# Self entries of a graph aggregation: 63 products on TensorE replaced by ten adds on GpSimd

## The reference, cut to what matters

```python
x, src, dst = ...                     # x [1250, 512]; 40000 edges, ids below 1250
def gnn(x, edge_index, W1, b1, W2, b2):
    h = relu(x @ W1 + b1) @ W2 + b2   # W1 [512, 256], W2 [256, 512]
    row, col = edge_index             # (src, dst)
    agg = segment_sum(h[col], row, num_segments=1250)
    return h + agg                    # h itself: the self entry of each node
def ffn(x, W_gate, b_gate, W_thr, b_thr, W_exp, b_exp):   # 8 experts of 512 x 512
    g = softmax(x @ W_gate + b_gate)
    w = g - 0.25 * sigmoid(x @ W_thr + b_thr)
    w = where(w >= 0, w, 0); w = w / sum(w)               # 1 where the sum is 0
    return sum_e w[:, e] * (x @ W_exp[e] + b_exp[e])
x = x + gnn(layernorm(x), (src, dst), ...)
x = x + ffn(layernorm(x), ...)
```

## Time and profile before

| | before |
|---|---|
| median of 3 runs | 352.44 us (351.34 to 352.58) |
| profiled execution | 352.29 us |
| its span, first to last instruction | 350.4 us |
| PE busy | 338.0 us, 96% |
| DVE busy | 296.0 us, 84% |
| ACT busy | 119.7 us, 34% |
| POOL busy | 83.6 us, 24% |
| mean granted TensorE clock | 0.995 of full |

### The profile page before, as it was taken

How to read it: one execution, slowest core, us unless ns; L and a number is a source line. 1 busy time by engine, 2 the same in 40 slices (tenths; PEclk the granted TensorE clock), 3 DMA queues, 4 the chain that set the end, 5 groups by cost and what they waited for, 6 DMA issues and landing times.

```text
span 350.4 us, 7647 instructions
## 1 busy us (share of the span) xinstructions
PE 338.0 (96%) x2637; PEld 263.4 (75%) x2637; DVE 296.0 (84%) x571; ACT 119.7 (34%) x233; POOL 83.6 (24%) x151
## 2 busy tenths in 40 slices
PE   8699999999999999899999999999999999999995
PEld 8599885655555545567668888888888888888884
DVE  7799999997896869977878888888889888898764
ACT  6898753454542026577313121030030210300000
POOL 5000032434343003437324060320500502200000
PEclk9989999999999999999999999999999999999999
DMA  8965132334433400040000030210300300000133
GB/s 179 254 162 173 43 83 59 74 80 93 89 86 85 135 0 0 0 127 3 0 0 2 2 120 3 59 64 2 120 3 2 120 2 2 1 2 0 60 116 121
DMA packets 20226, 22.09 MB, mean 63 GB/s; under 512 B 11850, under 2 KB 12647, under 8 KB 20188
## 3 DMA queue, kind: packets, MB, share of 16 engines
q1 hardware_dynamic: 17420, 18.36, 18.8%
q0 software_dynamic: 2352, 2.71, 3.4%
q10 hardware_dynamic: 416, 0.53, 0.7%
HBM read 12.77 MB, written 2.56 MB: 44 GB/s over the span
## 4 chain that ended last, share of the span: by engine, by line
PE 86%; DVE 7%; issue 2%; DMA 2%; ACT 1%; DVEq 0%; SPq 0%; ACTq 0%
PE ps_g L1195 12%; PE ps_g L1394 11%; PE ps_g L1395 11%; PE ps_g L1396 11%; PE ps_w L1255 8%; PE ps_g L1183 5%; PE ps_a L1394 2%; PE ps_a L1396 2%; PE ps_a L1395 2%; PE ps_g L1318 2%; PE ps_w L1394 2%; PE ps_w L1395 2%; PE ps_w L1396 2%; PE ps_w L1234 2%; PE ps_g L1360 2%
## 5 line engine op out<-in xcount | busy, mean ns | idle before, releaser
L1067 DVE SCALAR_TENSOR_TENSOR x_sb<-ps_g,weight_s,x_sb 125x256 f32<-125x256 f32 (+1 forms) x142 | 75.2, 547 | 19.5 <-PE ps_g L1396 18.4
L865 DVE TENSOR_TENSOR split<-places,keys 125x756 f16<-125x756 int16 (+4 forms) x119 | 73.2, 675 | 4.8 <-PE ps_w L1255 2.5
L1394 PE MATMUL ps_g<-wb_hi,places 128*128 128x256 f16 x212 | 57.8, 273 | 0.1
L1395 PE MATMUL ps_g<-wb_lo,places 128*128 128x256 f16 x212 | 57.8, 273 | 0.0
L1396 PE MATMUL ps_g<-wb_hi,r_sb 128*128 128x256 f16 x212 | 57.8, 273 | 0.0
L1195 PE MATMUL ps_g<-late,r_sb 125*128 125x512 f32 (+3 forms) x120 | 51.7, 534 | 0.9 <-DMA late<-counts 0.9
L401 POOL DMA_DIRECT2D late<-counts x49 | 28.3, 577 | 80.5 <-ACT counts L599 80.0
L1255 PEld LDWEIGHTS ps_w<-split 125*128 125x128 f16 x476 | 29.9, 98 | 13.8 <-issue 6.4
L1394 PE MATMUL ps_g<-wb_hi,split 128*128 128x256 f16 x142 | 38.7, 273 | 0.0
L1396 PE MATMUL ps_g<-wb_hi,split 128*128 128x256 f16 x142 | 38.7, 273 | 0.0
L1395 PE MATMUL ps_g<-wb_lo,split 128*128 128x256 f16 x142 | 38.7, 273 | 0.0
(11 more groups left out here) (232 smaller groups left out, 679.5 us busy)
## 6 DMA issues: line engine op xcount, KB each, us to landing
stage<-in_L_ffn_W_exp_dram SPq DMA_DIRECT2D x8, 1024.0 KB, 5.2
late<-counts SPq DMA_DIRECT2D x54, 58.6 KB
late<-counts POOLq DMA_DIRECT2D x41, 58.6 KB, 2.8
x_sb<-in_x_dram SPq DMA_DIRECT2D x5, 448.0 KB, 11.2
out_dram<-x_sb SPq DMA_DIRECT2D x10, 224.0 KB
w_sb<-in_L_gnn_W_dram SPq DMA_DIRECT2D x2, 512.0 KB, 10.9
out_dram<-x_sb ACTq DMA_DIRECT2D x10, 26.0 KB
b_sb<-in_L_gnn_b_dram SPq DMA_DIRECT2D x1, 250.0 KB
```

The costliest lines, as they stand in the source:

```text
L865: nc.vector.tensor_tensor(hot[hot_at(stage, p)][:, 0:n, :].rearrange("p c (k x j) -> p c k x j", k=SEGS, j=2), places_of(windows[s], n), k ...
L1067: nc.vector.scalar_tensor_tensor(out=x_sb[:, i, a:z], in0=bank[0:R, at:at + z - a], scalar=weight_s[:, expert_of(u), i:i + 1], in1=x_sb[:, ...
L1394: nc.tensor.matmul(out_cols, hi_x, wb_hi[par][:, q, k, :], start=(opens and k == 0), stop=False, skip_group_check=True)
L1395: nc.tensor.matmul(out_cols, hi_x, wb_lo[par][:, q, k, :], start=False, stop=False, skip_group_check=True)
```

## The change

The bank of a group is opened by a product of zeros with one column, which only marks it as fresh (`clear`), and no self entries are counted. When a tile's rows have landed, GpSimd adds the identity to the 125 x 125 block of the tile that lies on the diagonal (`add_self`), for tiles 0 to 8 behind its own moves of group LAST[i] + 2 (tile 0: group 8), for tile 9 behind all moves. Cut 0 and `column_sum` wait for this add (`self_added`) in place of the landings; for tile 9 only cut 2, which holds the diagonal block, waits for it, and comes after cut 3. The constants `self_pos` and `self_lo` go.

```diff
-        self_pos = sb("self_pos", [128, 128 + HI - 1], F16)
-        self_lo = sb("self_lo", [128, 3 * LO + 2 * WIN], F16)
-        zeros = sb("zeros", [1, BANK], F16)
+        zeros = sb("zeros", [128, 128], F16)
+        SELF_LAG = 2
@@ GpSimd
-            nc.gpsimd.memset(zeros[:, :], 0.0).then_inc(self_ready, 1)
-            nc.gpsimd.memset(self_pos[:, :], 0.0).then_inc(self_base, 1)
-            nc.gpsimd.memset(self_lo[:, :], 0.0).then_inc(self_base, 1)
-            pool.wait_ge(self_base, 2)
-            pool.wait_ge(const_ready, CONSTS)
-            nc.gpsimd.tensor_tensor(self_pos[...], ident[...], ident[...], ALU.add).then_inc(self_ready, 1)
+            nc.gpsimd.memset(zeros[:, :], 0.0).then_inc(zeros_ready, 1)
+
+            def add_self(i):
+                moved(pool, i)
+                own = a_t[i % 3][:, i * R:(i + 1) * R]
+                nc.gpsimd.tensor_tensor(own, own, ident[0:R, 0:R], ALU.add).then_inc(self_added, 1)
...
+            SELF_AT = {max(LAST[i] + SELF_LAG, POOL_MOVES): i for i in range(TILES - 1)}
+            pool.wait_ge(const_ready, CONSTS)
             begun = [2]
             for g in range(POOL_MOVES, NG):
                 pool.wait_ge(win_out, g + 1)
                 move(pool, g, 1, begun)
+                if g in SELF_AT:
+                    add_self(SELF_AT[g])
+            add_self(TILES - 1)
@@ ScalarE
-            act.wait_ge(self_base, 2)
             act.wait_ge(const_ready, CONSTS)
-            for a in (0, WIN):
-                at = LO if a == 0 else 2 * LO + WIN
-                nc.scalar.activation(self_lo[...], ident[...], ACT.Copy).then_inc(self_ready, 1)
@@ VectorE
             def column_sum(i):
-                moved(dve, i)
+                dve.wait_ge(self_added, i + 1)
@@ TensorE
             def aggregate(i, first, last, closes=None):
                 if first == 0:
-                    moved(pe, i)
+                    pe.wait_ge(self_added, i + 1)
...
-            def self_entries(g, pieces):
...
+            def clear(g, pieces):
+                empty = nc.tensor.matmul(ps_w[g % 2][:, 0:1], zeros[:, :], zeros[:, 0:1], start=True, stop=False, skip_group_check=True)
                 if g > 0 and g - 1 not in pieces and (g > SLOTTED or last_step_of(g - 1) % SLOT_STEPS > 0):
-                    own.then_inc(win_done, 1)
-                if not whole:
-                    ...
+                    empty.then_inc(win_done, 1)
...
-                self_entries(g, pieces)
+                clear(g, pieces)
...
-            pe.wait_ge(self_ready, 4)
+            pe.wait_ge(zeros_ready, 1)
...
             moved(pe, TILES - 1)
-            begin = (0, 2, 3)
+            begin = (0, 3, 2)
             for n in begin:
+                if n == 2:
+                    pe.wait_ge(self_added, TILES)
                 g = cut(TILES - 1, n)
```

More of the change, by code:

```diff
@@ L252, in gnn_moe @@
         places_ready, pads_ready = sem("places_ready"), sem("pads_ready")
-        self_base, self_ready = sem("self_base"), sem("self_ready")
+        zeros_ready, self_added = sem("zeros_ready"), sem("self_added")
         keys_placed = sem("keys_placed")
@@ L504, in _ @@
             group_rows(fill, (row_inv, "inv"), (row_size, "size"), (row_base, "base"))
-            nc.gpsimd.memset(zeros[:, :], 0.0).then_inc(self_ready, 1)
-            nc.gpsimd.memset(self_pos[:, :], 0.0).then_inc(self_base, 1)
-            nc.gpsimd.memset(self_lo[:, :], 0.0).then_inc(self_base, 1)
-            pool.wait_ge(self_base, 2)
-            pool.wait_ge(const_ready, CONSTS)
-            nc.gpsimd.tensor_tensor(self_pos[0:2 * WIN, HI - 1 + SHIFT:HI - 1 + SHIFT + POS].rearrange("p (r h) -> p r h", h=HI)[:, :, 0],
-                                    ident[0:2 * WIN, 0:WIN], ident[0:2 * WIN, WIN:2 * WIN], ALU.add).then_inc(self_ready, 1)
+            nc.gpsimd.memset(zeros[:, :], 0.0).then_inc(zeros_ready, 1)
[3 more added lines that the diff above has]
+                nc.gpsimd.tensor_tensor(own, own, ident[0:R, 0:R], ALU.add).then_inc(self_added, 1)
             def block_sums(e):
@@ L524, in block_sums @@
                 nc.gpsimd.tensor_tensor(t_sum[:, T4 - T1, :, :], b21, t_sum[:, T2 - T1, :, :], ALU.subtract).then_inc(t_added, 1)
+            SELF_AT = {max(LAST[i] + SELF_LAG, POOL_MOVES): i for i in range(TILES - 1)}
+            assert len(SELF_AT) == TILES - 1 and max(SELF_AT) < NG
+            pool.wait_ge(const_ready, CONSTS)
             begun = [2]
@@ L616, in _ @@
                 table(k)
-            act.wait_ge(self_base, 2)
             act.wait_ge(const_ready, CONSTS)
-            for a in (0, WIN):
-                at = LO if a == 0 else 2 * LO + WIN
-                nc.scalar.activation(self_lo[0:2 * WIN, at:at + WIN], ident[0:2 * WIN, a:a + WIN], ACT.Copy).then_inc(self_ready, 1)
             key_view = keys[:, FRONT * REC:(FRONT + CH) * REC].rearrange("p (c t) -> p c t", t=REC)
@@ L1223, in slot_behind @@
                         turn_x(k + XTS)
-            def self_entries(g, pieces):
[L1227 to L1235, removed]
-                if g > 0 and g - 1 not in pieces and (g > SLOTTED or last_step_of(g - 1) % SLOT_STEPS > 0):
-                    own.then_inc(win_done, 1)
-                if not whole:
-                    a = 0 if rows <= WIN else LO
-                    nc.tensor.matmul(bank[:, a:cols], self_pos[:, HI - 2 - tile:HI - 2 - tile + 128],
-                                     self_lo[:, 2 * LO - at + a:2 * LO - at + cols], start=False, stop=False, skip_group_check=True)
+            def clear(g, pieces):
+                empty = nc.tensor.matmul(ps_w[g % 2][:, 0:1], zeros[:, :], zeros[:, 0:1], start=True, stop=False, skip_group_check=True)
+                if g > 0 and g - 1 not in pieces and (g > SLOTTED or last_step_of(g - 1) % SLOT_STEPS > 0):
+                    empty.then_inc(win_done, 1)
             def count(g, pieces):
```

## The result

The changed kernel is slower: median 356.06 us (355.9 to 356.33, 5 runs) against 352.44 us, ratio 1.0114 with a 95% interval of 1.01 to 1.0128. That is outside the range, and on the other side than forecast. Its profiled execution has a span of 354.3 us where before had 350.4.

What follows compares the result with a forecast made beforehand. TensorE was taken as the bound, with VectorE close behind. Removing products gives 3.15 us, less 0.95 and 0.2 for waits at tiles 4 and 5: 2.0 us, so 350.4 us against 352.44; range 349.2 to 353.0.

Steps and rivals of the forecast that it cites:

- tile 0's add: GpSimd in group 12: issued at about 46.9, waits out L922's 1.48 us, delays VectorE's next step 0.35 us; net gain 0.
- the rule that an add costs: GpSimd's adds: each costs VectorE up to 0.35 us and itself up to one step more, 0.66 us at group 12.
- Rival (c): Adds of tiles 4 to 8 starve behind VectorE's back-to-back steps, 5.5 us on TensorE's path: 355.9 us; chance 0.09.
- The removal of the products: TensorE from 52.8 us on: dropping the self-entry products saves 3.15 us, before the waits for adds are taken off.
- The 0.25 us taken off behind cuts of 512 columns: TensorE: work beside the fixed path falls from 1.47 to 1.36 us, just under it, so 0.25 us less gain over all.
- the one-column product: TensorE, opening each group's bank: taken at 0.057 us from L1342's rows, against 0.11 for L1234 in an ordinary group.
- Rival (b): The one-column product costs a full 0.11 us in ordinary groups, so 1.35 us saved: 351.1 us; chance 0.13.
- the removal gives nothing before 52.8 us: Groups 0 to 12: TensorE would save 1.2 us but VectorE never rests, so 0, between -0.3 and +0.3.
- The wait at tile 4: TensorE's first cut of tile 4 waits 1.1 us for landing plus add, 0.15 of it waited already: costs 0.95.
- Tile 5: TensorE's first cut of tile 5 waits for the add, ready at 90.0: costs 0.2 us.
- tile 9's add: In the tail: ready at about 117.8, hidden by a microsecond behind cuts 0 and 3, so it costs nothing.
- Rival (d): VectorE bounds groups 24 to 31 and 12, as adds cost it extra: 1 to 2 us back, 351.4 to 352.4; chance 0.17.

Runs made afterwards that it cites:

- e8: The kernel before with one GpSimd add of 125 x 125 on scratch behind GpSimd's move of group 8, nobody waiting for it: 351.83 us, ratio 1.0014.
- e2: The changed kernel with a VectorE memset of 512 columns of scratch behind each of the two L923 passes: 350.84 us, ratio 0.9971.
- e5: The changed kernel with a VectorE add of two SBUF inputs, 512 columns on scratch, behind each of the two L923 passes: 357.08 us, ratio 1.0137.
- e10: The changed kernel with each of the ten adds replaced by a GpSimd memset on scratch, same waits, self entries left out: 348.88 us, ratio 0.9906.
- e9: The kernel before with one GpSimd add on scratch behind the move of group 8, first waiting until tile 0 has landed: 357.2 us, ratio 1.0139.
- e7: The changed kernel with 18 products of ones on TensorE just ahead of its first wait for an add: 353.53 us, ratio 1.0037.
- e3: The changed kernel without the ten adds, waiting for landings as before the change, self entries left out: 348.72 us, ratio 0.9914.
- e6: The changed kernel with a one-column VectorE memset behind the one-hot steps of each group from 8 on: 349.68 us, ratio 0.9938.
- e11: The changed kernel with a one-column VectorE memset behind the one-hot steps of groups 8 to 29 only: 349.54 us, ratio 0.9924.

## Why the prediction was wrong

**The step that failed** is the one on tile 0's add: "it is issued at about 46.9, sits out the 1.48 us of L922 and then holds up the next step by its own length, 0.35 us", and with it the rule that an add costs "itself up to one step (0.66 us at group 12) more". I took it that the two engines take turns, from two pairs of instructions; there they did, and so did e8's add. Tile 0's was issued at 46.24 and sat out L923 and the 12 steps and the other L923 behind it, 10.93 us in place of under 2. VectorE's row was in the earlier trace rows, 12.80 busy of 12.80 us; I used it only for what the add would cost VectorE, not for when GpSimd would get in. e2 and e5 show that it waits for VectorE's two-input row, e10 that an instruction without reads doesn't, and e9 that neither the landed rows nor TensorE's wait is needed for it.

**Rival (c)** named the mechanism, an add that starves behind VectorE's back-to-back steps, and its 355.9 us lie beside the measured 356.06. That is luck in the number: it put the starving at tiles 4 to 8, where the adds took 0.40 to 0.74 us, and didn't price tile 0, nor the clock. It had a chance of 0.09. The reason against it, that VectorE is idle while it waits for the same add, did hold for tile 4; at tile 5 VectorE was in its last step and waited 0.34 us behind it. It is also a reason why one starved add was all: the adds of tiles 2 and 3 (70.60 and 78.07 us) came less than 0.6 us before VectorE stopped for a column sum that waits for them.

**The lowered clock** was in no part of the prediction: 2.25 us, shown by e7. The wait of 4.88 us on TensorE was dearer by this than its length.

**The removal of the products** came out right in sum: 3.15 us forecast, 3.1 measured (e3). Part of that is luck, since terms in it were off. The 0.25 us taken off behind cuts of 512 columns have no ground in the earlier trace rows: the work there, 1.36 us, is longer than the path from 92.64 to 93.88, which is 1.24. At tile 4 e3 waits 0.38 us for the bare landing, which the 3.15 don't hold. And the one-column product was too dear: it starts 0.03 us ahead of the first one-hot product, not 0.057, as the timeline of the changed kernel shows:

```profile
72.00 0.17 PE L1228 MATMUL ps_w<-zeros 128*128 128x1 f16 x1
72.03 0.60 PE L1244 MATMUL ps_w<-split 125*128 125x125 f16 x8
```

Rival (b), a one-column product at the full 0.11 us, is out. The weight load's length, which spoke for it, doesn't set the spacing: L1342's loads are longer (0.14 us) than L1234's (0.10), and still four of its products take 0.23 us. What took back what the cheaper product gave isn't shown; the waits behind the short cuts, which from 84.79 us on end with VectorE in e3, are the likely place.

**That the removal gives nothing before 52.8 us** was right: TensorE waited for VectorE in group 12, and the first cut of e3 came 0.09 us earlier.

**The wait at tile 4** was right in place and nearly in size: forecast 1.1 us, measured 0.81 in the changed kernel and in e2, and 0.89 in e6. With 0.38 of it in e3 too, the add itself accounts for about 0.4. The chain of the changed kernel has landing, add and cut in a row:

```profile
84.43 3.34 DMA late<-counts
87.77 0.41 POOL late L510
88.22 1.13 PE ps_g L1196 x2
```

The add is 0.41 us where 0.35 was taken. Tile 5 didn't wait (0.2 forecast); tile 9's add hid, as forecast, though it took 1.38 us.

**Rival (d)**, VectorE as the bound, showed late in the stage (waits of 0.48, 0.48 and 0.53 us for one-hots at 98.79, 105.69 and 112.64), but e3 has waits of the same size without any add, so it isn't the adds that cost them.

The forecast of 350.4 us is near what the change brings where no add starves: e11 has 349.54.

## What to carry to other kernels

Before work is put on GpSimd, look at what VectorE does at the moment when it arrives, not at what both do on the average: a GpSimd instruction that reads SBUF can be held off for as long as VectorE's two-input instructions follow each other without a pause, here for 11 us, though at another moment it may get in. If it is on the path, put a VectorE instruction that reads nothing where it arrives (a memset of 128 x 512 let it in here, and with memsets of one column no add starved), or let another engine do it; and price a long wait on TensorE with the lowered clock behind it, here 2.25 us behind one of 4.88.

## What was not expected of the hardware

The two engines don't always take turns: an add that takes 0.40 us when VectorE is idle took 10.93, 11.38, 11.50, 11.61 and 12.55 us in five kernels, and ended 0.26 to 0.31 us behind VectorE's last two-input instruction in each of these traces. Other adds got in behind the one such instruction that they met (0.70 us for tile 7 of the changed kernel, 0.98 in e8). A memset of GpSimd beside the same VectorE instructions took 0.20 us.

The Trainium skill ("SBUF — State Buffer", section "Who interferes with whom") says that a VectorE instruction with two SBUF inputs contends with a GpSimd instruction that reads SBUF, not with one that only writes, and, of VectorE's two-port modes, that "Whoever issues first gets the shared pair for the whole instruction" while the other blocks. The runs agree on which instructions meet (12.55 us in e5, 0.20 in e10), and show in addition that the end of one instruction need not let the other in.

In 4.88 us without a product TensorE's granted clock went from 1.00 to 0.50, and with 18 products of no use ahead of the wait, which kept it at 1.00, the kernel was 2.5 us faster.
